# A message-passing layer on one core: 200 binned groups with folded units, one load a unit, and fewer passes on ScalarE

## The chip, the core and the metric
One core of a Trainium2 chip runs the whole kernel in one launch. The metric is the device time of the execution in microseconds; the median of three runs of the kernel before is 1935.99 us.

## The reference
A graph with N = 6250 nodes of 64 features and E = 206250 edges, sorted by their target `dst`; `src` is in no order. Each edge takes the node features of its `dst` and its own 64 features through two layers of 128, and the result is summed over the edges of each `src`:

```python
h = concatenate([hx[dst], edge_attr], axis=1)        # hx = relu(layernorm(x))
h = relu(h @ W1.T + b1)
h = relu(h @ W2.T + b2)
agg = segment_sum(h, src, n) / maximum(segment_sum(1, src, n), 1)[:, None]
z = relu(concatenate([hx, agg, u], axis=1) @ Wa.T + ba)
return x + z @ Wb.T + bb
```

## The kernel before, in words
**Before the loop** the nodes' part of the first layer is computed for all nodes and stored in DRAM as `p_table`; edge indices are brought into the forms that the loop reads.

**The loop** goes over 403 groups of 512 edges (four tiles of 128), one a step. For group s, `R[:, s % 8, :]` has the edges' features in its upper 64 partitions and, in the lower 64, a one-hot of the target among 64 neighbouring rows; `L[:, s % 8, :]` holds the weights and these 64 rows of `p_table`. The first layer is one fp32 matmul of 512 columns (two records in the trace, L1373) into `psL1`. ScalarE applies the ReLU (L923). In step s + 1 come four matmuls of the second layer (L1399) onto a bias seeded by ScalarE (L912), and its ReLU (L943).

What follows depends on the kind of group. There are 211 **plain** groups. VectorE builds a mask of equal sources (L1182, from rows of sources that SP loads, `src<-rows_src`), TensorE multiplies it in step s + 2 (L1389), so that each edge holds the sum over its tile's edges of the same source; ScalarE evacuates into one of four buffers `scat` (L931), once the scatters of the plain group four back have landed; VectorE sets the indices (L1187, L1190), and GpSimd issues four indirect DMAs that add rows into one of four sets `sums` in DRAM (L821). Each waits for the previous one into its set.

The 192 **binned** groups are the odd ones from 3 to 385. A source belongs to one of 49 bins (its remainder by 49); a tile has four places for each bin and 60 places for what overflows. The placement comes from a one-hot of bins (L1175), a rank matmul (L1417, `psRank`), VectorE's L1154, L1156, L1160, L1163, two small matmuls (L1432, L1434, `psOver`) and L1140 into `perm`. In step s + 2 TensorE places each tile's edges with two matmuls (`bin_tile`, L1350), tiles 0 and 1 before the second layer of the next group and tiles 2 and 3 behind it; ScalarE evacuates each tile by itself (`evac_slots`, L906) into `slot_sb`. SP stores it (L606, L607) into `slots[n, place, :]`. The overflow rows of two binned groups are added up (L1204, L1205, `V`, L1410, L1170, L1423, L965) and go out in one indirect DMA (L809), 96 in all.

**Units.** The binned groups form blocks of 32 (six blocks). A unit is two bins of one block, 25 units a block. SP loads it (L629), one DMA a bin: 128 partitions (32 groups x 4 places) of four tiles x 130 values. VectorE makes a one-hot of each row's source, one operation a bin and tile (L1215, `oh2`), TensorE multiplies (`add_up`, L1361, eight matmuls, 16 records) and VectorE adds the result into `acc` (`add_unit`, L1131 for the first block, L1134 for the others). `unit_steps` gives the steps: for blocks 0 to 4 one unit at an even step, 25 spread over the steps to the next block's first unit (64 steps, for the last of them 60); the first is nine steps behind the last group of its block (step 74 for block 0). Block 5 runs from step 390, three units one a step and then two a step to 403. A unit of step s is loaded in SP's step s (one later in the last block), its one-hots are made in VectorE's step s - 1, and it is added in VectorE's step s + 1. Loads go into three buffers, six in the last block (`BX`, in space that is free by then).

**The destination one-hot** is made on VectorE for plain groups (L1147, one operation, step s - 1). For binned groups ScalarE makes it in two passes (L954, the absolute value of the difference, and L959, ReLU of one minus it, step s - 2).

**The order** on every engine is the program's order, written by hand as one function `step(s)` for each, and engines wait for one another by semaphores. On TensorE a step is: first layer of s, sum or tiles 0 and 1 of s - 2, second layer of s - 1, tiles 2 and 3, the matmuls for the overflow rows and ranks, the unit, the two small matmuls for the overflow places. On VectorE: L1140, L1147, ranks and places, L1170, L1175, L1182, indices, L1204 and L1205, the add of the unit before, the one-hots of the next.

**The finish.** When all scatters have landed SP and ScalarE load the four sets in pieces (`regA<-sums`), VectorE adds them and `acc` (L1231, L1233, L1234), and the update layers and the store follow. TensorE first waits for all units' adds and then issues the node features' part of the update layer (L1452).

The branch `general == 1` is for inputs that break the assumptions on windows and places; with these inputs it is not taken.

Of the kernel before, what the change touches and what calls it, by code (L numbers as in the profile page):

```python
# [5 lines left out]
P = 128  # L6
TILE = 128
TPG = 4
# [39 lines left out]
LAST_SORTED = 386  # L48
# [9 lines left out]
BLOCK = 32  # L58
QLAG, VPRE, VREAD, VBC, VMASK, VSUM, VLAG = 6, 3, 7, 6, 7, 8, 5
ODD = 196  # L60
NS = ODD * TPG
# [3 lines left out]
ROUNDS = [[(0, 4), (4, 5)]] + [[(a, a + 4), (a + 4, a + 8)] for a in range(5, 45, 8)] + [[(45, 49)]]  # L65
# [8 lines left out]
UNIT_RING, SPARE = 3, 3  # L74
TAIL_LAG, TAIL_LEAD = 5, 1


def is_sorted(g):
    return 2 < g < LAST_SORTED and g % 2 == 1

# [11 lines left out]
BLOCKS = [BINNED[k:k + BLOCK] for k in range(0, NH, BLOCK)]  # L92
# [42 lines left out]
def unit_steps():  # L135
    at = {}
    firsts = [block[-1] + VREAD + 2 for block in BLOCKS[:-1]] + [BLOCKS[-1][-1] + TAIL_LAG]
    for k in range(len(BLOCKS) - 1):
        for q in range(UNITS):
            span = firsts[k + 1] - firsts[k]  # L140
            s = firsts[k] + 2 * (span * q // (2 * UNITS))
            at.setdefault(s, []).append((k, q))
    alone = VSUM - TAIL_LAG
    for q in range(UNITS):
        s = firsts[-1] + (q if q < alone else alone + (q - alone) // 2)
        at.setdefault(s, []).append((len(BLOCKS) - 1, q))
    return at
# [3 lines left out]
STEPS = max(max(UNITS_AT) + TAIL_LEAD + 1, NG + VSUM + 1)  # L151
# [5 lines left out]
UNIT_NO = {kq: n for n, kq in enumerate(kq for s in sorted(UNITS_AT) for kq in UNITS_AT[s])}  # L157


LOADS_AT = {}  # L160
for at, units in sorted(UNITS_AT.items()):
    for k, q in units:
        LOADS_AT.setdefault(at + (TAIL_LEAD if k == len(BLOCKS) - 1 else 0), []).append((k, q))
TAIL_UNIT = len(UNIT_NO) - UNITS
PAIRED = TAIL_UNIT + VSUM - TAIL_LAG


def buffer_of(m):
    return m % UNIT_RING if m < TAIL_UNIT else (m - TAIL_UNIT) % (UNIT_RING + SPARE)


def users(m):
    return [n for n in range(m + 1) if buffer_of(n) == buffer_of(m)]


def added_for(m):
    return m if m <= PAIRED else m - 1
# [6 lines left out]
def arrived(m):  # L184
    parts = {n: unit_bins(q)[1] for (_, q), n in UNIT_NO.items()}
    return sum(parts[n] for n in users(m))


# [8 lines left out]
def build(nc, x, src_cols, dst_cols, src_rows, dst_rows, ea, u, w1t, b1, w2t, b2, wat, ba, wbt, bb, out):  # L197
# [13 lines left out]
    with ctx:  # L211
# [67 lines left out]
        def loaded(m):  # L279

            n = buffer_of(m)
            return BR[:, n, :, :, :] if n < UNIT_RING else BX[:, n - UNIT_RING, :, :, :]
# [1244 lines left out]
```

## Time and profile before
| what | us |
|---|---|
| median of three runs | 1935.99 |
| lowest, highest | 1925.9, 1936.51 |
| span of the profiled execution | 1917.2 |
| busy in it: TensorE | 1737.8 |
| ScalarE | 1433.6 |
| VectorE | 1289.0 |
| GpSimd | 1528.8 |

The profile is of one execution; the page gives its span from the first to the last instruction, and no time of its own beside it. The median of the runs is 18.8 us above the span. PE is TensorE's matmul, PEld its weight load, DVE VectorE, ACT ScalarE, POOL GpSimd, SP the engine that issues most DMAs. In rows, `<-` leads from what is written to what is read, and behind a time of idleness to what ended it. An fp32 matmul shows as two records, and a few records can be missing.

### The profile page before, as it was taken

How to read it: one execution, taken by the hardware profiler on the slowest of the kernel's cores; microseconds unless marked ns; L12 is line 12 of the kernel's file. 1: busy time of each engine (PE TensorE's matmuls, PEld its weight loads, DVE VectorE, ACT ScalarE, POOL GpSimd, SP SyncE). 2: the span in 40 equal slices, each digit the busy share in tenths (PEclk: the TensorE clock that was granted, in tenths of full speed). 3: DMA queues.
4: the chain of work that ended last, by engine and by line, in shares of the span. 5: the costliest groups of instructions: out<-in, count | busy, mean ns of one | idle time of the engine just before them, and what ended most of it. 6: DMA issues, size and time to landing. Idle time of an engine off the chain costs nothing.

```text
span 1917.2 us, 43265 instructions
## 1 busy us (share of the span) xinstructions
PE 1737.8 (91%) x12472; PEld 1470.5 (77%) x12472; DVE 1289.0 (67%) x4235; ACT 1433.6 (75%) x2975; POOL 1528.8 (80%) x991
## 2 busy tenths in 40 slices
PE   6898888999999999999999999999999999978837
PEld 4677666888888888888788788888888888867725
DVE  8565555667767676777776777777776676756727
ACT  4788887878888877788788787878877877862306
POOL 8488888888888888888888888888888888888850
PEclk8999999999999999999999999999999999998969
DMA  9988888999999999999999999999999999999856
GB/s 329 269 166 151 151 151 149 187 198 193 198 192 192 201 190 196 201 192 192 200 197 187 185 199 198 200 193 197 204 194 198 191 199 199 197 183 234 176 116 217
DMA packets 319400, 372.10 MB, mean 194 GB/s; under 512 B 42272, under 2 KB 203264, under 8 KB 318528
## 3 DMA queue, kind: packets, MB, share of 16 engines
q1 hardware_dynamic: 182400, 305.12, 55.6%
q0 software_dynamic: 135360, 62.15, 34.4%
q8 instruction: 110, 1.80, 0.4%
q10 hardware_dynamic: 1408, 2.03, 0.3%
q14 instruction: 122, 1.00, 0.1%
HBM read 203.87 MB, written 159.27 MB: 189 GB/s over the span
## 4 chain that ended last, share of the span: by engine, by line
POOL 44%; issue 19%; PE 17%; DMA 11%; DVE 5%; ACT 3%; SPq 1%; ACTq 0%; POOLq 0%; DVEq 0%
POOL sums L821 39%; DMA sums<-regA,idx 7%; POOL sums L809 5%; PE bank L1361 4%; PE bank L1350 4%; PE bank L1399 3%; PE bank L1373 3%; DVE regC L1215 2%; PE bank L1389 1%; DMA regC<-slots 1%; DMA regA<-sums 1%; DMA sums<-vscat,vidx 1%; ACT regA L931 1%; DVE regC L1182 1%; PE bank L1275 1%
## 5 line engine op out<-in xcount | busy, mean ns | idle before, releaser
L821 POOL DMA_INDIRECT sums<-regA,idx x844 | 1333.9, 1580 | 291.7 <-issue 244.4
L1350 PEld LDWEIGHTS bank<-h,regC 128*128 128x128 f32 x3072 | 389.0, 194 | 183.1 <-ACT h L943 134.0
L1350 PE MATMUL bank<-h,regC 128*128 128x130 f32 x3072 | 421.7, 281 | 63.0 <-ACT h L943 62.8
L1373 PE MATMUL bank<-regA,L 128*128 128x512 f32 x806 | 435.8, 623 | 4.6 <-DVE regA L1147 3.0
L1399 PE MATMUL bank<-w,h 128*128 128x128 f32 x3224 | 431.3, 277 | 0.0
L923 ACT ACTIVATE h<-bank,b1c 128x512 f32<-128x512 f32 x403 | 275.7, 684 | 198.0 <-PE bank L1373 193.1
L1399 PEld LDWEIGHTS bank<-w,h 128*128 128x128 f32 x3224 | 398.0, 194 | 1.1 <-ACT h L923 0.6
L1215 DVE TENSOR_SCALAR regC<-lows,regC 128x128 f32<-128x128 f32 x1176 | 257.7, 315 | 147.6 <-DMA regC<-slots 124.0
L1361 PE MATMUL bank<-regC 128*128 128x129 f32 x2352 | 298.3, 281 | 34.4 <-issue 19.0
L943 ACT ACTIVATE h<-bank 128x512 f32<-128x512 f32 x403 | 240.9, 598 | 111.1 <-PE bank L1399 107.2
L1361 PEld LDWEIGHTS bank<-regC 128*128 128x128 f32 x2352 | 277.2, 193 | 41.8 <-issue 38.1
L1389 PEld LDWEIGHTS bank<-h,regC 128*128 128x128 f32 x1688 | 223.1, 192 | 102.2 <-issue 98.7
L906 ACT ACTIVATE regC<-bank 128x260 f32<-128x260 f32 x768 | 270.4, 385 | 4.5 <-PE bank L1350 3.9
L912 ACT ACTIVATE bank<-b2b 128x512 f32<-128x512 f32 x403 | 242.4, 602 | 11.2
L1389 PE MATMUL bank<-h,regC 128*128 128x130 f32 x1688 | 224.7, 276 | 0.5 <-ACT h L943 0.5
L1182 DVE TENSOR_TENSOR regC<-src,srcF 128x512 f32<-128x512 uint16 x211 | 146.4, 694 | 99.7 <-DMA src<-rows_src 95.1
L1156 DVE TENSOR_TENSOR regC<-bank,ranks 128x784 f32<-128x784 f32 x192 | 184.5, 961 | 0.0
L931 ACT ACTIVATE regA<-bank 128x520 f32<-128x520 f32 x211 | 126.4, 599 | 71.7 <-DMA sums<-regA,idx 54.6
L809 POOL DMA_INDIRECT sums<-vscat,vidx x96 | 153.0, 1594 | 31.2 <-issue 26.8
L1154 DVE TENSOR_REDUCE rank<-bank 128x4 f32<-128x196 f32 x192 | 68.3, 356 | 140.0 <-PE bank L1417 137.6
L1140 DVE TENSOR_TENSOR regC<-bank,overs 128x240 f32<-128x240 f32 x192 | 77.0, 401 | 115.8 <-PE bank L1434 114.9
L954 ACT ACTIVATE regA<-dstR,oh_bias 64x512 f32<-64x512 uint8 x192 | 137.6, 717 | 4.9
(142 smaller groups left out, 1540.3 us busy)
## 6 DMA issues: line engine op xcount, KB each, us to landing
regC<-slots SPq DMA_DIRECT2D x294, 260.0 KB, 5.6
regA<-in_ea SPq DMA_DIRECT2D x202, 256.0 KB
slots<-regC SPq DMA_DIRECT2D x192, 260.0 KB
src<-rows_src SPq DMA_DIRECT2D x107, 256.0 KB
slots<-regC SPq DMA_DIRECT2D x192, 138.1 KB
sums<-regA,idx POOLq DMA_INDIRECT x844
dstR<-rows_dst SPq DMA_DIRECT2D x101, 128.0 KB
sums<-zeros SPq DMA_DIRECT2D x20, 645.0 KB, 7.0
```

The lines of the kernel that those rows point to most:

```text
L809: nc.gpsimd.indirect_dma_start(out=sums[k], out_offset=bass.IndirectOffsetOnAxis(ap=vidx[:, j % 6:j % 6 + 1], axis=0), in_=vscat[:, j % 4, ...
L821: nc.gpsimd.indirect_dma_start(out=sums[k], out_offset=bass.IndirectOffsetOnAxis(ap=idx[:, n % RING, t:t + 1], axis=0), in_=scat[:, n % 4, ...
L906: nc.scalar.activation(slot_sb[:, n % 2, :, t, :], psSlot(t), ACT.Copy).then_inc(slot_ready, 1)
L912: nc.scalar.activation(psL2(g % 2).rearrange("p (t f) -> p t f", t=TPG), b2b[:, :].unsqueeze(1).broadcast_to([P, TPG, H]), ACT.Copy).then_ ...
L923: nc.scalar.activation(h1[:, s % 2, :], psL1(s % 2), ACT.Relu, bias=b1c[:, :]).then_inc(h1_ready, 1)
L943: nc.scalar.activation(h2[:, g % 2, :, 0:H], psL2(g % 2).rearrange("p (t f) -> p t f", t=TPG), ACT.Relu).then_inc(h2_ready, 1)
L1215: made = VE.tensor_scalar(oh2[0:rows, m % 2, i, t, :], lows[0:rows, i, :], loaded(m)[0:rows, i, t, C:W], -float(b), ALU.subtract, ALU.is_e ...
L1350: last = T.matmul(psSlot(t)[:, k, :], place, h2[:, g % 2, t, :], start=True, stop=True)
L1361: last = T.matmul(psUnit(m)[:, i * C:(i + 1) * C], oh2[0:rows, m % 2, i, t, :] if not general else zeros[0:rows, 0:LO], loaded(m)[0:rows, ...
L1373: T.matmul(psL1(s % 2), L[:, s % RING, :], R[:, s % RING, :], start=True, stop=True).then_inc(l1_done, 1)
L1389: last = T.matmul(bank[:, 6 + t // 2, (t % 2) * W:(t % 2 + 1) * W], S[:, n % 4, t, :], h2[:, g % 2, t, :], start=True, stop=True)
L1399: last = T.matmul(psL2(g % 2)[:, t * H:(t + 1) * H], h1[:, g % 2, t * TILE:(t + 1) * TILE], w2[:, :], start=False, stop=True, skip_group_c ...
```

## The change
- Binned are now the 200 odd groups from 3 to 401; 203 groups stay plain.
- Blocks are of 32 groups (four), 16 (four) and 8 (one). `FOLD` is 1, 2 and 4: the tiles of a row are folded onto partitions, so a unit of a smaller block again has 128 partitions, with two tiles or one behind each, and takes half or a quarter of the matmuls. There are 225 units.
- `unit_steps`: blocks 0 to 2 as before. From block 3 on units follow one another: a whole unit takes two steps, a half one a step, a quarter half a step, and none starts ahead of its block. So block 3 has steps 266 to 315, the four half blocks 316 to 415, the last block 416 to 428. The last two blocks are loaded a step later than the others.
- `slots` is laid out by bin, then by group and place, so that a unit's rows are contiguous, and one DMA loads both bins. The three buffers are a ring of 12 quarters; `BX` is gone.
- The unit's one-hot is one operation with two tensor operands for all tiles of a bin, two a unit.
- ScalarE evacuates two tiles of a binned group in one pass over two banks, and TensorE's third tile waits for the first pass.
- The destination one-hot is VectorE's for all groups; ScalarE's two passes go.
- Units' sums lie in one bank until step 404 and then in four in turn.

```diff
-LAST_SORTED = 386
+FIRST_SORTED, LAST_SORTED = 3, 402
...
-BLOCK = 32
+SIZES = [32] * 4 + [16] * 4 + [8]
...
-UNIT_RING, SPARE = 3, 3
-TAIL_LAG, TAIL_LEAD = 5, 1
+UNIT_RING = 3
+LATE, LATE_LAG, STEADY = 2, 5, 3
...
+BLOCKS = [BINNED[sum(SIZES[:k]):sum(SIZES[:k + 1])] for k in range(len(SIZES))]
+FOLD = [max(SIZES) // len(block) for block in BLOCKS]
...
+    late = len(BLOCKS) - LATE
+    firsts = [block[-1] + (VREAD + 2 if k < late else LATE_LAG) for k, block in enumerate(BLOCKS)]
+    for k in range(STEADY):
         for q in range(UNITS):
             span = firsts[k + 1] - firsts[k]
...
+            at.setdefault(firsts[k] + 2 * (span * q // (2 * UNITS)), []).append((k, q))
+    due = 4 * firsts[STEADY]
+    for k in range(STEADY, len(BLOCKS)):
+        due = max(due, 4 * firsts[k])
+        for q in range(UNITS):
+            at.setdefault(due // 4, []).append((k, q))
+            due += 8 // FOLD[k]
...
+APART = NG + 2
+ALONE = sum(len(units) for s, units in UNITS_AT.items() if s < APART)
...
+            at.setdefault(s + (1 if k >= len(BLOCKS) - LATE else 0), []).append((k, q))
...
-    slots = nc.dram_tensor("slots", (NH, PLACES, TPG * W), f32, kind="Internal").ap()
+    slots = nc.dram_tensor("slots", (NBIN, NH * CAP, TPG * W), f32, kind="Internal").ap()
...
-            return bank[:, 0 if m >= PAIRED and m % 2 else 1, 0:PAIR * C]
+            return bank[:, 1 if m < ALONE else 2 + (m - ALONE) % 4, 0:PAIR * C]
...
-                    sp.dma_start(slots[n, 0:HEAD, :], slot_sb[OVER:P, n % 2, 0, :, :].rearrange("p t c -> p (t c)")).then_inc(slot_out[n % 2], 16)
+                    sp.dma_start(slots[0:HEAD // CAP, CAP * n:CAP * (n + 1), :], slot_sb[OVER:P, n % 2, 0, :, :].rearrange("p t c -> p (t c)")).then_inc(slot_out[n % 2], 16)
...
-                    for i in range(nb):
-                        sp.dma_start(loaded(m)[0:CAP * len(block), i, :, :].rearrange("p t c -> p (t c)"),
-                                     slots[h0:h0 + len(block), CAP * (b + i):CAP * (b + i + 1), :]).then_inc(unit_in[buffer_of(m)], 16)
+                    wait(sp, unit_done, UNIT_FREED[m])
+                    r0, r1 = (CAP * FOLD[k] * h for h in (BINNED_NO[block[0]], BINNED_NO[block[-1]] + 1))
+                    folded = slots[b:b + nb, :, :].rearrange("b r (f x) -> (r f) b x", f=FOLD[k])
+                    sp.dma_start(loaded(m)[0:r1 - r0, 0:nb, :, :].rearrange("p b t c -> p b (t c)"), folded[r0:r1, :, :]).then_inc(unit_in[UNIT_AT[m]], 16)
...
+            def evac_slots(g, pair):
+
+                n, t = BINNED_NO[g], 2 * pair
+                act.wait_ge(slot_done, TPG * n + t + 2)
...
-                nc.scalar.activation(slot_sb[:, n % 2, :, t, :], psSlot(t), ACT.Copy).then_inc(slot_ready, 1)
+                nc.scalar.activation(slot_sb[:, n % 2, :, t:t + 2, :].rearrange("p h t c -> p t h c"), psSlots, ACT.Copy).then_inc(slot_ready, 1)
...
-                    nc.scalar.activation(R[D:P, g % RING, :], dB[D:P, i % 2, g % GPP, :], ACT.Abs, bias=oh_bias[D:P, :]).then_inc(oh_far, 1)
...
-                    nc.scalar.activation(R[D:P, g % RING, :], R[D:P, g % RING, :], ACT.Relu, bias=1.0, scale=-1.0).then_inc(oh_act_ready, 1)
...
-                if 0 <= g < NG and not is_sorted(g):
+                if 0 <= g < NG:
...
-                        for t in range(TPG):
-                            made = VE.tensor_scalar(oh2[0:rows, m % 2, i, t, :], lows[0:rows, i, :], loaded(m)[0:rows, i, t, C:W], -float(b), ALU.subtract, ALU.is_equal)
+                        made = VE.scalar_tensor_tensor(out=oh2[0:rows, m % 2, i, 0:size, :], in0=loaded(m)[0:rows, i, :, C:W].broadcast_to([rows, size, LO]), scalar=float(b),
+                                                       in1=lows[0:rows, i, :].unsqueeze(1).broadcast_to([rows, size, LO]), op0=ALU.subtract, op1=ALU.is_equal)
...
-                if t >= 2:
-                    pe.wait_ge(slot_ready, TPG * n + t - 1)
+                if t == 2:
+                    pe.wait_ge(slot_ready, 2 * n + 1)
...
-                wait(pe, acc_ready, added_for(m))
+                wait(pe, acc_ready, m if m < ALONE else m - 3)
```

## Rows read from the trace of the kernel before

**Rows 1.** The head of the page.
```profile
span 1917.2 us, 43265 instructions
```

**Rows 2.** The chain of waits, 1000 to 1060 us: start us, us, what.
```profile
1013.75 1.54 POOL sums L821
...
1015.60 1.55 POOL sums L821
```

**Rows 3.** Groups by line, whole span: count, busy us, mean ns, idle before.
```profile
L821 POOL DMA_INDIRECT sums<-regA,idx x844 | 1333.9, 1580 | 291.7 <-issue 244.4 <-DVE idx L1190 25.5 <-DMA sums<-regA,idx 12.8
...
L906 ACT ACTIVATE regC<-bank 128x260 f32<-128x260 f32 x768 | 270.4, 385 | 4.5 <-PE bank L1350 3.9
L1215 DVE TENSOR_SCALAR regC<-lows,regC 128x128 f32<-128x128 f32 x1176 | 257.7, 315 | 147.6 <-DMA regC<-slots 124.0 <-PE bank L1361 22.9
...
L1182 DVE TENSOR_TENSOR regC<-src,srcF 128x512 f32<-128x512 uint16 x211 | 146.4, 694 | 99.7 <-DMA src<-rows_src 95.1
L954 ACT ACTIVATE regA<-dstR,oh_bias 64x512 f32<-64x512 uint8 x192 | 137.6, 717 | 4.9
L931 ACT ACTIVATE regA<-bank 128x520 f32<-128x520 f32 x211 | 126.4, 599 | 71.7 <-DMA sums<-regA,idx 54.6 <-PE bank L1389 12.7 <-DMA sums<-vscat,vidx 3.3
...
L959 ACT ACTIVATE regA<-regA 64x512 f32<-64x512 f32 x192 | 120.3, 627 | 4.6
L1147 DVE TENSOR_SCALAR regA<-dstR,oh_row 64x512 f32<-64x512 uint8 x211 | 109.7, 520 | 31.1 <-DMA dstR<-rows_dst 24.4
...
L1205 DVE TENSOR_TENSOR vpre<-vhalf 60x130 f32<-60x130 f32 x192 | 55.3, 288 | 6.6
L1134 DVE TENSOR_TENSOR regB<-regB,bank 128x258 f32<-128x258 f32 (+1 forms) x125 | 51.3, 417 | 2.0 <-PE bank L1361 2.0
```

**Rows 4.** Windows: PE, PEld, DVE, ACT, POOL busy us (count), PEclk, DMA share, GB/s.
```profile
100.00:350.00 250.00, 214.91 (x1459) 175.73 (x1460) 135.76 (x413) 205.46 (x433) 209.47 (x134) 0.96 0.84 154
350.00:1700.00 1350.00, 1300.03 (x9619) 1117.67 (x9618) 959.63 (x3293) 1088.57 (x2270) 1124.05 (x712) 0.99 0.94 196
```

**Rows 5.** Waits of the vector engine, 350 to 1700 us: us in total, times, longest.
```profile
DVE regC L1215 <- DMA regC<-slots: 108.6, 88, 3.2
DVE regC L1140 <- PE bank L1434: 106.2, 84, 2.4
DVE regC L1182 <- DMA src<-rows_src: 89.1, 61, 3.1
DVE rank L1154 <- PE bank L1417: 35.6, 35, 2.8
```

**Rows 6.** Timeline of PE over one pair of steps: start us, us, what.
```profile
999.99 1.05 PE L1373 MATMUL bank<-regA,L 128*128 128x512 f32 x2
...
1002.66 1.95 PE L1361 MATMUL bank<-regC 128*128 128x129 f32 x16
1004.45 0.17 PE L1432 MATMUL bank<-over,prefix 128*128 128x4 bf16 x1
...
1008.46 1.02 PE L1373 MATMUL bank<-regA,L 128*128 128x512 f32 x2
```

**Rows 7.** Timeline of the end of the scatters and the start of the finish.
```profile
1830.08 0.60 ACT L931 ACTIVATE regA<-bank 128x520 f32<-128x520 f32 x1 [3.27 <-PE bank L1389]
...
1832.14 5.33 PE L1452 MATMUL bank<-hT,wax 128*128 128x256 f32 x16 [2.11 <-issue]
...
1853.86 1.54 POOL L821 DMA_INDIRECT sums<-regA,idx  x1 [0.30 <-issue]
...
1862.34 1.23 DVE L1231 TENSOR_TENSOR regC<-regA 128x1032 f32<-128x1032 f32 x1 [31.21 <-DMA regA<-sums]
```

**Rows 8.** DMA queue q1, 1100 to 1600 us: packets, MB, share of 16 engines.
```profile
q1 hardware_dynamic: 50591, 80.43, 57.0%
```

**Rows 9.** The same queue, 1864 to 1870 us, sums loaded alone.
```profile
q1 hardware_dynamic: 596, 2.16, 95.1%
```

**Rows 10.** The same queue, 1905 to 1917 us, output stored alone.
```profile
q1 hardware_dynamic: 720, 0.56, 14.2%
```

More of the change, by code:

```diff
@@ L176, in added_for, with load_steps, ring_table @@
-def added_for(m):
-    return m if m <= PAIRED else m - 1
+UNIT_OF = {n: kq for kq, n in UNIT_NO.items()}
+APART = NG + 2
+ALONE = sum(len(units) for s, units in UNITS_AT.items() if s < APART)
+def load_steps():
+    at = {}
+    for s, units in sorted(UNITS_AT.items()):
+        for k, q in units:
+            at.setdefault(s + (1 if k >= len(BLOCKS) - LATE else 0), []).append((k, q))
+    return at
+LOADS_AT = load_steps()
+QUARTERS = UNIT_RING * TPG
+def ring_table():
+    place, freed, arrived, at = {}, {}, {}, 0
+    last, begun = {}, [0] * QUARTERS
+    for m in range(len(UNIT_OF)):
+        k, q = UNIT_OF[m]
+        size = TPG // FOLD[k]
+        mine = range(at, at + size)
+        place[m] = at
+        freed[m] = max((last[c] + 1 for c in mine if c in last), default=0)
+        for c in mine:
+            last[c] = m
+        begun[at] += 1
+        arrived[m] = begun[at]
+        at = (at + size) % QUARTERS
+    return place, freed, arrived
@@ L197, in build @@
+assert HEAD % CAP == 0 and LO * NBIN == NKEPT >= N and OVER + PLACES == PW and 2 * OVER <= P and NH == 2 * NV and NG + max(VSUM, VLAG) < STEPS and NH == sum(SIZES)
+assert NBIN == BA * BA and PACK * BA <= P and NS == NPACK * PACK and PARTS[-1][1] == NPACK and (FIRST_SORTED - 1) * TPG + 2 * NS <= NT and all(len(units) == 1 for s, units in UNITS_AT.items() if s < APART)
 def build(nc, x, src_cols, dst_cols, src_rows, dst_rows, ea, u, w1t, b1, w2t, b2, wat, ba, wbt, bb, out):
@@ L584, in _ @@
                         i = s // GPP
-                        wait(sp, oh_ready, sum(1 for g in range(GPP * (i - 1)) if not is_sorted(g)))
-                        wait(sp, oh_act_ready, sum(1 for g in range(GPP * (i - 1)) if is_sorted(g)))
+                        wait(sp, oh_ready, GPP * (i - 1))
                         sp.dma_start(dB[D:P, i % 2, :, :].rearrange("p b e -> p (b e)"), rows_dst[i].partition_broadcast(P - D)).then_inc(dB_in[i % 2], 16)
@@ L1366, in step @@
                 if s < NG:
-                    pe.wait_ge(oh_ready, sum(1 for g in range(s + 1) if not is_sorted(g)))
-                    wait(pe, oh_act_ready, sum(1 for g in range(s + 1) if is_sorted(g)))
+                    pe.wait_ge(oh_ready, s + 1)
                     pe.wait_ge(ea_in[(s // 2) % 4], 16 * (s // RING + 1))
```

102 lines of the change are left out of this document (27 added, 75 removed).

## The prediction

> **What bounds the kernel now.** I read the head of the page first [rows 1]: one profiled execution with a span of 1917.2 us. The page gives no time of that execution beside the span, so I take the 18.8 us between it and the median of the three runs shown (1935.99) as what lies around it; the runs spread over 10.6 us. Then the chain of waits. It shows GpSimd's indirect accumulating DMAs one behind the other: one starts at 1013.75 and the next at 1015.60, so a scatter costs 1.85 us of GpSimd (1.54 busy and 0.30 that the profile calls issue) [rows 2]. The groups by line count 844 of them at L821 [rows 3]; with the 96 of L809 there are 940, and 940 x 1.85 = 1739 us of the 1917. A pair of steps (one plain group, one binned) has 4 + 1/2 scatters, so GpSimd alone asks 4.5 x 1.85 = 8.33 us for it. The windows show whether the loop runs at that [rows 4]: before any unit is added, 134 scatters in 250 us are 29.8 pairs of 8.40 us; with units 712 in 1350 us are 158.2 pairs of 8.53 us. There TensorE is busy 1300 of 1350 us, VectorE 960 and ScalarE 1089. So GpSimd sets the pace, 0.2 us a pair is lost to others, and TensorE is nearly as full, which matters as soon as the change gives it more.
>
> The waits of the vector engine say how it stands in the same stretch [rows 5]: 108.6 us for units' loads and 89.1 for source rows, that is 197.7 / 158.2 = 1.25 us a pair for DMAs, and 106.2 + 35.6 for TensorE, 0.90 a pair. Its own work is 959.6 / 158.2 = 6.07.
>
> TensorE's timeline over one pair [rows 6] goes from one L1373 at 999.99 to the second next at 1008.46: 8.47 us without a visible hole, with one unit in it (1002.66 to 1004.45, 1.79 us). A block of 32 spreads 25 units over 32 pairs, 0.78 a pair, so the average content is 8.47 - 0.22 x 1.79 = 8.08.
>
> **The change, part by part.**
> Eight plain groups become binned: 8 x 4 scatters go and 4 per-pair scatters come, 28 fewer, 28 x 1.85 = 51.8 us off GpSimd [rows 2]. This is the gain. The last plain sum is evacuated at 1830.08 and the last scatter ends at 1853.86 + 1.54 = 1855.4, 25.3 us later [rows 7]; after the change these stand at 1803.6 and 1778.3 if nothing else becomes late. The finish begins on VectorE at 1862.34, 6.9 us behind the last scatter, and lasts 54.8 us; that part is not changed.
>
> The tail of units. By the step table the 25 units of the first block of 16s run from step 316, one a step, and so on; those of the fourth run from 391 to 415, those of the block of 8 two a step from 416 to 428, while the edges end at 402. Behind the evacuation of the last plain sum (step 404) some 12 half units and 25 quarter units remain. I price a unit on VectorE: two one-hot operations and one add of 0.417 (L1134) [rows 3]. The new one-hot has two tensor operands; the nearest row for 512 elements is L1182 with 694 ns, for 256 L1134 with 417, for 128 L1205 with 288. A whole unit is then 2 x 0.694 + 0.417 = 1.81, a half one 1.25, a quarter one 0.99. TensorE needs 0.9 and 0.45 for the last two, so VectorE paces the tail: 12 x 1.25 + 25 x 0.99 = 40 us, with 3 for the first and last links. It ends at 1778.3 + 43 = 1821.5, where the scatters would have let the finish begin at 1803.6 + 6.9 = 1810.5: 11 us given back. The bounds are 0 (the units keep up with the 25 us of scatters) and 30 (each unit also waits for its load). The first matmuls of the finish on the node features, 5.33 us at 1832.14 [rows 7], lay under the scatters and now follow the last unit: I add 1.
>
> The dense stretch. The whole units of block 4 run one a pair from step 266 to 316 and the half units two a pair to 402, 25 + 43.5 = 68.5 pairs with one unit's worth of matmuls each instead of 0.78. TensorE's content rises from 8.08 to 8.47 [rows 6], now above GpSimd's 8.33. From below, a pair costs 8.47, less than today's 8.53; from above, today's whole distance of pace and content (0.45) stays and it costs 8.92. I take 8.8, nearer the upper end, because two engines with the same load don't hide each other's jitter: (8.8 - 8.53) x 68.5 = 18.5 us, between -4 and +27. The eight more binned groups are within these pairs.
>
> ScalarE loses both passes of the destination one-hots (717 + 627 ns, 192 times, 258 us) and evacuates slots in 400 passes of about 0.6 (L931 is the same shape of read) for 768 that were busy 270 [rows 3]: 30 us less. It was not what bound, so most of that is worth nothing. What it may give is part of the 0.2 us a pair lost between steps 74 and 266 (96 pairs): between 0 and 19 us, I take 6. The new evacuation waits for two tiles instead of one; behind it in ScalarE's queue stand h2's evacuation and then the second pair, and TensorE's third tile waits for the first pair. The second layer's matmuls between tiles two and three (as many as half a unit's, 0.9 us) cover its 0.6, with little to spare; if not, the loss is up to 0.1 us a pair, and it lies in the upper bound above.
>
> VectorE takes the destination one-hots of the binned groups: 200 x 0.520 (L1147) = 104 us. A whole unit's one-hots go from 8 x 0.219 = 1.75 (257.7 / 1176) to 1.39. Over all: one-hots 196 x 0.694 + 196 x 0.417 + 49 x 0.288 = 232 us instead of 257.7, and 75 more adds of 0.417, 31 us. VectorE ends near 1400 us busy, hidden beside GpSimd and TensorE as long as a pair leaves it room. In the half-unit stretch its work is 6.07 - 0.78 x 2.17 + 0.52 + 2 x 1.25 = 7.40 us of 8.8.
>
> The Trainium skill speaks against the one-hot edit (VectorE: DVE Perf Modes, section The perf-mode tier table): an fp32 operation with a scalar on SBUF runs at two elements a cycle and one with two tensors at one, so folding four of the first into one of the second throws the faster mode away. By the cost table of that page (section The TRN2 errata) I estimate (58 + 64) / 0.96 = 127 ns for the old operation, 1.0 us for eight, and a whole unit would cost VectorE 0.37 us more than before instead of 0.36 less. The trace has the old operation at 219 ns, so the row decides, and at neither price does VectorE pass TensorE.
>
> The loads. One DMA of two bins replaces two; SP issues 225 instead of 294, and none of its waits is new, apart from the late blocks, whose first load stands one step behind the last slot store. A folded load moves half (or a quarter) of the bytes in packets of 1040 (or 520) bytes instead of 2080. Does a packet cost by its bytes? Queue q1 took 57.0% x 500 x 16 / 50591 = 90 ns for 1590 bytes in the loop [rows 8], 95.1% x 6 x 16 / 596 = 153 ns for 3.6 KB alone [rows 9] and 14.2% x 12 x 16 / 720 = 38 ns for 0.78 KB alone [rows 10]: by its bytes, nearly. So the fold costs nothing, and 0.22 more units a pair add (0.94 - 0.84) / 0.78 x 0.22 = 0.03 to a DMA share of 0.94 [rows 4]. The other bound is a rival below. The new layout of the slots keeps each row of 2080 bytes whole; I take nothing. The eight more prologue tiles cost below 1 us.
>
> **The sum.** 1917.2 - 51.8 + 11 + 1 + 18.5 - 6 = 1889.9 of span, and 18.8 around it: 1909 us.
>
> **The rivals.**
> A: GpSimd still paces the whole loop and TensorE's extra hides, because its holes are taken from waits for the scatters (evacuations wait for landings at L931). Then only the tail counts: 1917.2 - 51.8 + 12 = 1877, time 1896, and with all of ScalarE's relief (19) 1877. For it speaks that the loop without units runs at 8.40, against it that TensorE has 50 us of holes in 1350.
> B, slower: VectorE becomes the bound in the half-unit stretch. TensorE's unit of a step waits for the add of the unit before, which stands last but one in VectorE's step, behind the destination one-hot it has been given. If its waits are latencies of loads and of rank matmuls that stay as they are, a pair costs 7.40 + 1.25 + 0.90 = 9.55: 43.5 x 1.02 = 44 us, with 7 for the 25 pairs before them. 1917.2 - 51.8 + 12 + 51 = 1928, time 1947. It passes today's time when a half-unit pair costs over 9.28. Against it: such waits shrink when VectorE comes later.
> C, slower: a packet under load costs 90 ns whatever its size. 2 x 256 packets a pair for 0.78 x 256 are 312 more, 312 x 0.09 / 16 = 1.8 us onto a DMA load of 0.94 x 8.53 = 8.0: 9.8 a pair, 43.5 x 1.27 + 7 = 62, time about 1958. Rows 9 and 10 speak against it.
>
> **How the numbers follow.** My sum 0.45, A 0.26, B 0.20, C 0.09. A change of about 1% (19 us) is what a measurement of this kernel can tell from none. My sum has +/-15 of its own around 1909, so two thirds of it is faster by over 1% (0.30); with A that is 0.56. The other third, half of B and a third of C are within 1%: 0.26. The rest, 0.18, is slower. The range takes in most of A and the foot of B and C: 1880 to 1952.
>
> **What would show it.** Right: 912 scatters 1.85 apart, L954, L959 gone, L1147 with 403 instructions of 0.52; the last scatter near 1804 to 1822; behind it a stretch with VectorE near full and units only; L1215 at 694, about 420 and 290 ns; pairs of 8.4 to 8.5 us before step 266 and of 8.7 to 8.9 behind it. Wrong: pairs over 9.2 with long waits of L1215 for slots (B, C; C with q1 over 70 ns for its smaller packets), or a pace that never leaves 8.5 (A), or a tail beyond 60 us between the last edge step and the finish.

## The result: 403 us slower, through one line of the layout

The changed kernel takes 2334.4 us (median of four runs, 2333.1 to 2335.3) beside 1931.2 (1925.9 to 1936.5) for the kernel before: a ratio of 1.2105, 95% interval 1.207 to 1.214. I had forecast 1909. The profiled execution took 2334.44 us for a span of 2332.4, so 2 us lie around the span.

The page of the changed kernel: head and busy times, two rows of the DMA part, the chain that ended last, and groups.

```profile
span 2332.4 us, 42606 instructions
...
PE 1913.0 (82%) x12676; PEld 1572.2 (67%) x12676; DVE 1404.9 (60%) x3823; ACT 1171.6 (50%) x2226; POOL 1486.0 (64%) x963
...
q1 hardware_dynamic: 201120, 310.57, 44.6%
...
SPq 53%; DMA 22%; PE 10%; issue 7%; DVE 7%; ACT 1%; DVEq 0%; ACTq 0%
...
L824 POOL DMA_INDIRECT sums<-regA,idx x812 | 1280.3, 1577 | 307.9 <-issue 276.1
...
L909 ACT ACTIVATE regC<-bank 128x520 f32<-128x520 f32 x400 | 241.6, 604 | 428.1 <-DMA slots<-regC 237.5
L812 POOL DMA_INDIRECT sums<-vscat,vidx x100 | 164.8, 1648 | 451.7 <-ACT vscat L955 417.2
L1203 DVE SCALAR_TENSOR_TENSOR regC<-regC,lows 128x512 f32<-128x512 f32 (+2 forms) x441 | 212.3, 524 | 393.7 <-DMA regC<-slots 393.3
...
L1136 DVE TENSOR_SCALAR regA<-dstR,oh_row 64x512 f32<-64x512 uint8 x403 | 208.7, 518 | 287.2 <-DMA dstR<-rows_dst 276.8
```

The edits did what they say: 912 scatters, no ScalarE passes for one-hots, 403 one-hots on VectorE at 0.52 us, as in [rows 3]. No engine is full. Every engine waits for DMAs: VectorE 393 us for units' loads and 277 for targets, ScalarE 238 for the slot stores. The chain, which before ran through GpSimd's scatters [rows 2], is now more than half "SPq": SyncE's issuing. Yet the DMA engines look idler than before. The window over the loop, changed kernel:

```profile
core 0: us, PE busy (x) PEld busy (x) DVE busy (x) ACT busy (x) POOL busy (x), PEclk, DMA share, GB/s
350.00:1780.00 1430.00, 1192.28 (x8099) 987.61 (x8098) 844.51 (x2295) 727.96 (x1384) 940.33 (x594) 0.96 0.74 156
```

594 scatters at 4.5 a pair are 132 pairs of 10.83 us, at a mean DMA share of 0.74. The kernel before had 8.53 us at 0.94 [rows 4]. A queue that holds up its issuer while the mean engine is a quarter idle suggests that the work is uneven. The view of one tile, `slots`, shows where. Changed kernel (ns min/median/max of an issue):

```profile
L613 SPq DMA_DIRECT2D slots<-regC x200: 629/729/779, 77.2 to 2227.0; - x100
L614 SPq DMA_DIRECT2D slots<-regC x200: 553/3209/5394, 78.0 to 2227.7; - x100
...
DMA to landing us min/median/max: 2.0/9.5/13.5
```

and the kernel before:

```profile
L606 SPq DMA_DIRECT2D slots<-regC x192: 298/508/1296, 76.9 to 1715.4; - x192
L607 SPq DMA_DIRECT2D slots<-regC x192: 338/349/1084, 77.4 to 1716.0; - x192
...
DMA to landing us min/median/max: 4.0/5.6/7.1
```

L613 is the first store, rows OVER to P, 68 of them, and L614 the second, of 128 rows. SyncE stays 3.2 us (median) in the issue of L614, once a pair, where the kernel before took 0.35 (L607). The timeline of SyncE in the changed kernel shows what stands behind:

```profile
1505.08 0.73 SPq L613 DMA_DIRECT2D slots<-regC  x1
1505.86 4.63 SPq L614 DMA_DIRECT2D slots<-regC  x1
1510.54 0.60 SPq L587 DMA_DIRECT2D regA<-in_ea  x1
```

The loads of edge features, targets and units all queue behind it.

**The theory** that the experiments test: the source of this store is 68 partitions, and its destination was 68 rows (`slots[n, 0:68, :]`) and is now 17 bins of 4 (`slots[0:17, 4n:4n+4, :]`). 17 and 68 have no common divisor up to 16 other than 1, so all 68 rows of 2080 bytes go through one of the 16 DMA engines. Before, 68 and 68 share 4. Bytes and rows of the store are the same. The Trainium skill states the rule (DMA: Bandwidth & Descriptors, section Why a DMA increments its semaphore by 16 and not by 1): the number of engines is the largest k up to 16 that divides the slowest dimension other than 1 of both sides. No view of the profile tells the 16 engines apart. The rivals: the new layout spreads the writes badly in DRAM whatever the number of engines; or the folded loads cost it (rival C of the prediction); or the loop has too many DMAs.

### The profile page after: what moved, and what is told of

Its sections match the earlier page's. It is cut to its first block, busy times and chain, and to the rows that moved or that the text cites. A ratio compares the mean times of both kernels' runs of the same rounds, so it can differ in the third digit from the quotient of the medians.

```text
span 2332.4 us, 42606 instructions
## 1 busy us (share of the span) xinstructions
PE 1913.0 (82%) x12676; PEld 1572.2 (67%) x12676; DVE 1404.9 (60%) x3823; ACT 1171.6 (50%) x2226; POOL 1486.0 (64%) x963
## 3 DMA queue, kind: packets, MB, share of 16 engines
q8 instruction: 113, 1.85, 0.3%
## 4 chain that ended last, share of the span: by engine, by line
SPq 53%; DMA 22%; PE 10%; issue 7%; DVE 7%; ACT 1%; DVEq 0%; ACTq 0%
SPq L614 17%; DMA regC<-slots 11%; SPq L599 9%; SPq L600 7%; DMA slots<-regC 7%; SPq L622 5%; SPq L587 4%; SPq L613 4%; DMA src<-rows_src 3%; SPq L633 3%; PE bank L1361 2%; PE bank L1350 2%; SPq L594 2%; SPq L606 2%; PE bank L1339 1%
## 5 line engine op out<-in xcount | busy, mean ns | idle before, releaser
L824 POOL DMA_INDIRECT sums<-regA,idx x812 | 1280.3, 1577 | 307.9 <-issue 276.1
L1339 PEld LDWEIGHTS bank<-h,regC 128*128 128x128 f32 x3200 | 410.5, 193 | 347.2 <-ACT regC L909 247.2
L1339 PE MATMUL bank<-h,regC 128*128 128x130 f32 x3200 | 451.9, 285 | 218.2 <-ACT regC L909 215.7
L1361 PE MATMUL bank<-regA,L 128*128 128x512 f32 x806 | 478.3, 678 | 7.6 <-DVE regA L1136 2.4
L909 ACT ACTIVATE regC<-bank 128x520 f32<-128x520 f32 x400 | 241.6, 604 | 428.1 <-DMA slots<-regC 237.5
L1203 DVE SCALAR_TENSOR_TENSOR regC<-regC,lows 128x512 f32<-128x512 f32 (+2 forms) x441 | 212.3, 524 | 393.7 <-DMA regC<-slots 393.3
L1136 DVE TENSOR_SCALAR regA<-dstR,oh_row 64x512 f32<-64x512 uint8 x403 | 208.7, 518 | 287.2 <-DMA dstR<-rows_dst 276.8
L1350 PE MATMUL bank<-regC 128*128 128x129 f32 x2450 | 327.7, 284 | 51.6 <-DVE regB L1123 32.4
L1350 PEld LDWEIGHTS bank<-regC 128*128 128x128 f32 x2450 | 301.7, 198 | 65.3 <-issue 48.5
L1377 PEld LDWEIGHTS bank<-h,regC 128*128 128x128 f32 x1624 | 245.3, 215 | 124.0 <-issue 117.1
L1377 PE MATMUL bank<-h,regC 128*128 128x130 f32 x1624 | 242.1, 297 | 0.0
L1361 PEld LDWEIGHTS bank<-regA,L 128*128 128x128 f32 x806 | 131.6, 205 | 23.8 <-issue 6.1
```

What stands on the lines that cost most here:

```text
L824: nc.gpsimd.indirect_dma_start(out=sums[k], out_offset=bass.IndirectOffsetOnAxis(ap=idx[:, n % RING, t:t + 1], axis=0), in_=scat[:, n % 4, ...
L909: nc.scalar.activation(slot_sb[:, n % 2, :, t:t + 2, :].rearrange("p h t c -> p t h c"), psSlots, ACT.Copy).then_inc(slot_ready, 1)
L1203: made = VE.scalar_tensor_tensor(out=oh2[0:rows, m % 2, i, 0:size, :], in0=loaded(m)[0:rows, i, :, C:W].broadcast_to([rows, size, LO]), sc ...
L1339: last = T.matmul(psSlot(t)[:, k, :], place, h2[:, g % 2, t, :], start=True, stop=True)
L1350: last = T.matmul(psUnit(m)[:, i * C:(i + 1) * C], oh2[0:rows, m % 2, i, t, :] if not general else zeros[0:rows, 0:LO], loaded(m)[0:rows, ...
L1361: T.matmul(psL1(s % 2), L[:, s % RING, :], R[:, s % RING, :], start=True, stop=True).then_inc(l1_done, 1)
```

## The experiments

Each time is a median beside the runs of the kernel before on the same chip (medians 1927 to 1931). I call the first one the repaired kernel; most others start from it. The cuts show the lines of the edit alone; where a third store is added, the waits for the stores' semaphore count 48 a pair in place of 32. Four to ten runs stand behind each median, and the runs of one kernel spread over 3 to 12 us (those of the kernel before over some 20). The repaired kernel and experiments 7, 9 and 13 ran on different chips, and the kernel before differs by up to 3 us between these chips. So a step of 11 us between two of them is more than either's spread, but the intervals of their ratios overlap.

**1. The changed kernel, first store in 16 bins and 1 bin.**
```diff
-sp.dma_start(slots[0:17, CAP * n:CAP * (n + 1), :], slot_sb[OVER:P, ...])
+sp.dma_start(slots[0:16, CAP * n:CAP * (n + 1), :], slot_sb[OVER:OVER + 64, ...])
+sp.dma_start(slots[16:17, CAP * n:CAP * (n + 1), :], slot_sb[OVER + 64:OVER + 68, ...])
```


> The changed kernel with its first slot store of 17 bins x 4 places cut into 16 bins and 1 bin, layout and everything else as changed. Theory 'one DMA engine' (17 bins against 68 partitions leave no common divisor of 16 or less, so the store's 68 rows all go through one of 16 DMA engines, which becomes the bound): the second store's 3.2 us on SP falls below 0.8, pairs of steps go from 11.2 us to 8.4 to 9.0, time 1890 to 1970. Rival 'layout' (four-row pieces 1.66 MB apart are slow to write or to issue in themselves): nothing moves, 2280 to 2350. Rival 'the other edits' (merged evacuation, VectorE's new work): also 2280 to 2350.

Measured: 1906.9 us, ratio 0.987 (0.983 to 0.992). 427.5 us go with one DMA more a pair. The tile `slots` of this kernel:

```profile
L614 SPq DMA_DIRECT2D slots<-regC x200: 490/520/581, 78.4 to 1809.5; - x100
L615 SPq DMA_DIRECT2D slots<-regC x200: 557/583/907, 79.0 to 1810.1; - x100
...
  DVE regC L1204: 4.1, 5
...
DMA to landing us min/median/max: 3.4/4.8/7.5
```

The issue behind the 16 bins takes 0.52 us, and VectorE's wait for units' loads is 4.1 us in all (before 124.0). So neither the layout in DRAM nor the folded loads nor the number of DMAs was the cause: both are in here, with one DMA more a pair.

**2. The changed kernel with the old layout of the slots** and two folded loads a unit:
```diff
-slots = nc.dram_tensor("slots", (NBIN, NH * CAP, TPG * W), ...)
+slots = nc.dram_tensor("slots", (NH, PLACES, TPG * W), ...)
...
-sp.dma_start(loaded(m)[0:r1 - r0, 0:nb, :, :]..., folded[r0:r1, :, :])
+for i in range(nb):
+    sp.dma_start(loaded(m)[0:rows, i, :, :]..., slots[h0:h0 + len(block), ...].rearrange("h r (f x) -> h (r f) x", f=FOLD[k]))
```


> The changed kernel with the slots laid out by group as before, stores as before, and so two loads a unit, folded from the old layout; all other edits kept. 'One DMA engine': the 68-row store is on 4 engines again, 1890 to 1970. 'Layout': the same, 1890 to 1970. 'The other edits': stays at 2280 to 2350.

Measured: 1975.8 us, 1.024 (1.020 to 1.029). The collapse is gone here too, but this is 69 us above the repaired kernel and 6 above the range on record; VectorE waits 152.5 us for units. Experiment 6 splits the 69.

**3. The kernel before, first store in 67 rows and 1.** Nothing else of the change is in it.
```diff
-sp.dma_start(slots[n, 0:HEAD, :], slot_sb[OVER:P, ...])
+sp.dma_start(slots[n, 0:67, :], slot_sb[OVER:OVER + 67, ...])
+sp.dma_start(slots[n, 67:68, :], slot_sb[OVER + 67:OVER + 68, ...])
```


> The kernel before with its first slot store of 68 rows cut into 67 rows and 1 row, old layout. 'One DMA engine': 67 has no divisor of 16 or less but 1, so 67 rows of 2080 bytes go through one engine, and the kernel before is slowed to 2200 to 2350, with the second store long on SP. 'Layout' and 'the other edits': one more small DMA a pair, 1930 to 1945.

Measured: 2324.6 us, 1.204 (1.199 to 1.209): 396 us, nearly the whole loss, made in the old layout by a number of rows that has no divisor up to 16 but 1. Its chain, the tile `slots` and the window over the loop repeat the picture:

```profile
SPq 72%; issue 9%; DMA 8%; PE 6%; POOL 3%; DVE 1%; ACT 1%; ACTq 0%; POOLq 0%; DVEq 0%
```
```profile
L606 SPq DMA_DIRECT2D slots<-regC x192: 272/470/514, 77.1 to 2112.3; - x192
L607 SPq DMA_DIRECT2D slots<-regC x192: 364/2904/4358, 77.6 to 2112.8; - x192
```
```profile
350.00:1780.00 1430.00, 1197.61 (x8069) 989.94 (x8068) 798.95 (x2734) 948.43 (x1923) 941.70 (x597) 0.96 0.73 155
```

**4. The kernel before, 64 rows and 4**, the same edit with other numbers, for the price of the extra DMA and of more even engines.

> The kernel before with its first slot store cut into 64 rows and 4 rows. 'One DMA engine', in its general form: 68 rows went through 4 engines, 17 rows each; now 4 each plus 1 on four of them, so the DMA waits of VectorE fall and the time is between 1 per cent faster and the same, 1912 to 1932. 'Layout' and 'the other edits': one more issue, 1930 to 1945.

Measured: 1921.0 us, 0.996 (0.993 to 0.998). A third store costs nothing; 64 rows on 16 engines for 68 on 4 give about 8 us.

**5. The kernel before, 47 rows and 21.** By the theory 47 rows go to one engine and 21 to seven, three each: 50 rows on the fullest if both DMAs begin at the same engine (and 68 in experiment 3). That they do is stated by the same section of the Trainium skill for this kind of queue; no run here shows it. The experiment tells "one engine is slow by its load" from "any such store is slow".

> The kernel before with its first slot store cut into 47 rows (one DMA engine) and 21 rows (7 engines, 3 each): the busiest engine carries 50 of these rows in place of 68. 'The engine's load is the bound': 67 rows made a pair of steps 10.6 us, of which 67 x about 0.09 are these packets, so 17 fewer take 1.5 us off, 9.1 a pair, 192 x 0.6 above the kernel before: 2020 to 2070. 'It is the mere use of one engine' (latency of the store or its issue, however many rows): 2200 to 2330.

Measured: 2042.6 us, 1.060 (1.054 to 1.066). It is the load:

```profile
L607 SPq DMA_DIRECT2D slots<-regC x192: 270/1068/2484, 78.5 to 1833.8; - x192
```

The traces count the engines more directly. Each part of a DMA that lands is recorded as an increment of its semaphore; the loop's loads of 64 and 128 rows, 16 engines by the rule, show 12.9 to 16.0 increments each, since some records are missing. All stores of a pair (that of 128 rows is always among them) show together:

| kernel | rows of the first store | increments a pair | by the rule |
|---|---|---|---|
| before | 68 to 68 | 20.7 | 4 + 1 + 16 = 21 |
| changed | 17 bins from 68 | 17.9 | 1 + 1 + 16 = 18 |
| repaired | 16 bins, 1 bin | 34.8 | 16 + 4 + 1 + 16 = 37 |
| experiment 3 | 67, 1 | 19.6 | 1 + 1 + 1 + 1 + 16 = 20 |
| experiment 4 | 64, 4 | 35.5 | 16 + 4 + 1 + 16 = 37 |
| experiment 5 | 47, 21 | 25.5 | 1 + 1 + 7 + 1 + 16 = 26 |

The last column takes one increment more for each store on fewer than 16 engines, which these counts suggest and nothing else here shows.

Over 192 pairs the excess is (2324.6 - 1928.3) / 192 = 2.06 us with 67 rows and (2042.6 - 1928.5) / 192 = 0.59 with 50. The 18 rows between 68 and 50 are 1.47 us, 82 ns a row (74 if the small part goes elsewhere and it is 67 against 47), near the 90 ns of a packet (of 1590 bytes in the mean) in the loop of before [rows 8]. Carried on as a straight line, the excess reaches zero near 43 rows; no run stands there. By this estimate the full engine spends 68 x 0.082 = 5.6 of a pair's 10.8 us on this store and has 5.2 for the rest. The rest does not fit the DMA share: 0.74 x 10.83 = 8.0 us of packets' time a pair on the mean engine is more than 5.2. So a packet's time in the profile is not simply time taken from the engine, and what the full engine spends on its other packets is not shown.

The next runs price the other parts, each undone alone in the repaired kernel (1906.9 us).

**6. One load a bin for one load a unit** (the loop over `i` of experiment 2, in the new layout).

> The run with 16 and 1 bins, with each unit loaded by one DMA a bin instead of one for both, from the same new layout. 'One load a unit is what took VectorE's wait for units away' (124 us before, 4 with it): the waits come back to over 100 us and the time goes to 1950 to 1980, like the run with the old layout. 'The contiguous layout did': waits stay below 30 us and time 1900 to 1920.

Measured: 1943.1 us, 1.008 (1.005 to 1.010): one load a unit is worth 36 us. I had it at nothing. The time lies between the ranges of the two theories, and so do VectorE's waits for units, 59.1 us (4.1 in the repaired kernel, 152.5 in experiment 2). Up to 1480 us the scatters are as many as in the repaired kernel (471 and 122 for 470 and 122 in 350 to 1250 and 1250 to 1480 us), and from 1480 to 1780 there are 141 for 150: the loss lies where the half units come. The other 33 us of experiment 2 belong to the old layout together with its first store in one piece of 68 rows; no run parts these two.

**7. One evacuation a tile for one a pair of tiles.**
```diff
-nc.scalar.activation(slot_sb[:, n % 2, :, t:t + 2, :]..., psSlots, ACT.Copy).then_inc(slot_ready, 1)
+nc.scalar.activation(slot_sb[:, n % 2, :, t, :], psSlot(t), ACT.Copy).then_inc(slot_ready, 1)
```


> The run with 16 and 1 bins, with ScalarE evacuating each tile of a binned group by itself as before (768 + 32 passes in place of 400). By my prediction this edit was worth nothing to speak of, since ScalarE doesn't bound: 1900 to 1915. Rival, the merged pass is a new wait of TensorE's third tile: 1885 to 1900. Rival, ScalarE's relief is what the gain rests on: above 1920.

Measured: 1895.8 us, 0.982 (0.976 to 0.988). The merged evacuation costs 11 us. In the whole run GpSimd waited 23.4 us for the evacuations of pair sums (`vscat`) in the repaired kernel and 5.7 here. ScalarE itself waited 86.5 us (301 times) for TensorE's tiles in front of the merged pass and 3.9 us (11 times) in front of the single ones. TensorE shows no wait of its third tile for ScalarE in either, so the time fell into the range of the rival, but the wait that the rival named is not the one that the rows show.

**8. The destination one-hots of binned groups on ScalarE again**, in two passes.

> The run with 16 and 1 bins, with the destination one-hots of binned groups on ScalarE again in two passes. Theory 'VectorE is near its bound in the half-unit stretch': taking 0.52 us a pair off it gives 5 to 25 us, 1882 to 1902. Rival 'ScalarE's latency holds the loop' (its freedom is what pays for the denser units): 1915 to 1940. By my sum (6 us): 1910 to 1918.

Measured: 1948.8 us, 1.010 (1.004 to 1.016). Taking them off ScalarE is worth 42 us, more than the range of the rival that had the direction right (1915 to 1940). The windows tell where; 1250 to 1480 and 1480 to 1780 us of the repaired kernel, then of this one:

```profile
1250.00:1480.00 230.00, 223.21 (x1684) 195.16 (x1683) 180.36 (x497) 145.27 (x274) 192.75 (x122) 1.00 0.96 205
1480.00:1780.00 300.00, 279.48 (x2074) 242.45 (x2073) 230.99 (x671) 181.61 (x337) 238.55 (x150) 1.00 0.91 192
```
```profile
1250.00:1480.00 230.00, 218.69 (x1612) 190.37 (x1612) 158.35 (x454) 175.11 (x313) 193.73 (x120) 0.99 0.94 197
1480.00:1780.00 300.00, 258.63 (x1841) 223.45 (x1839) 189.77 (x571) 202.56 (x357) 205.99 (x130) 0.96 0.82 171
```

Up to 1480 us the scatters are nearly as many (122, 120). Then, with a unit in every step, 150 become 130: a pair takes 10.4 us for 9.0. (The half units begin at 1399 us in the repaired kernel; its scatters run 33 us behind its first layer there.) The waits of this kernel between 1480 and 1780 us name it:

```profile
POOL sums L818 <- ACT vscat L972: 54.7, 13, 6.6
...
PEld bank L1368 <- ACT vscat L972: 40.2, 14, 2.9
PE bank L1368 <- ACT vscat L972: 37.5, 14, 2.7
```

The `vscat` evacuation stands last in ScalarE's step, behind both passes. GpSimd's scatter of the pair waits for it, and so does TensorE's unit. In the repaired kernel the same three waits are 19.1, 19.8 and 16.8 us. ScalarE is busy 203 us of 300: it is late and not full.

**9. The unit one-hots in one operation a tile again**, 1225 of them.
```diff
-made = VE.scalar_tensor_tensor(out=oh2[0:rows, m % 2, i, 0:size, :], ...)
+for t in range(size):
+    made = VE.tensor_scalar(oh2[0:rows, m % 2, i, t, :], lows[0:rows, i, :], loaded(m)[0:rows, i, t, C:W], ...)
```


> The first run of this study (the changed kernel with its first slot store in two, 1906.9 us) with one edit undone: the unit one-hots are again one operation per tile (0.219 us each in the kernel before) for one per bin (0.69, 0.42 and 0.29 us). By the rows 196 x 4 + 196 x 2 + 49 = 1225 of them are 268 us of VectorE for 214 us, 54 more. Theory: VectorE waits over 1 us a pair, so it has room and the pace stays: 1902 to 1918. Rival, VectorE is the bound wherever there are units, or TensorE's unit waits for the one-hots: most of the 54 us comes out, 1940 to 1960. Rival from the table of modes (an old operation 127 ns): VectorE has 156 us instead of 214, and if it bound, the time would fall to 1860 to 1890.

Measured: 1896.1 us, 0.982 (0.978 to 0.987), outside the range of every theory on record: VectorE has more to do (1477.8 us busy for 1409.3) and the kernel is 11 us faster.

**10. The kernel before with one part alone**, all destination one-hots on VectorE (and the store in 64 rows and 4).

> The kernel before with its first slot store in 64 and 4 rows (1921.0 us as an earlier run) and one part of the change alone: all destination one-hots on VectorE, both ScalarE passes gone. Theory: the relief was worth 42 us in the changed kernel only because there every step from 1450 us on has a unit, and TensorE's unit waits for ScalarE's evacuation of the pair sum behind the pass; in the kernel before both pace and count of scatters were the same with and without the passes up to 1480 us, so little comes here: 1908 to 1922. Rival, the passes delay ScalarE's evacuations everywhere, also where GpSimd waits for them: 42 us as there, 1875 to 1895.

Measured: 1923.0 us, 0.997 (0.995 to 1.000), beside 1921.0 without it. Alone the relief is worth nothing.

**11. The kernel before with the new layout, 16 bins and 1, and one load a unit.**

> The kernel before, blocks and everything else as they were, with the new layout of the slots (first store 16 bins and 1 bin) and one load for a unit's two bins: two parts of the change without the folding. Theory: VectorE's 149.5 us of waits for units' loads all but go, but these waits lie in room that it has while GpSimd and TensorE set the pace: 1908 to 1924 beside 1921.0 for the same kernel with the old layout and its store in 64 and 4 rows. The 36 us that one load was worth in the changed kernel belong to the stretch with units each step. Rival, one load is worth those 36 us in any kernel: 1880 to 1895.

Measured: 1912.6 us, 0.991 (0.989 to 0.994): 8 us less than experiment 4 (1921.0), for layout and single load together, though VectorE's waits for units fall from 149.5 to 11.7 us. Where units come in every step the single load alone is worth 36.

**12. The kernel of experiment 7 with the evacuation of the plain sum behind that of h2.**

> The fastest kernel so far (the changed one with its first store in two and one evacuation a tile, 1895.8 us) with ScalarE's evacuation of a plain sum moved behind the evacuation of h2 in its step. There it waits 161 us between 350 and 1100 us for scatters to land, and TensorE waits 109 us for the h2 evacuations queued behind it. Theory: those waits of TensorE are what a pair loses to GpSimd's 8.33 us (209 scatters in 400 us are 8.61 a pair), so half of 0.28 us over 190 pairs comes back: 1860 to 1885. Rival, GpSimd then waits for the plain sum, which comes later by h2's evacuation of 0.6 us, or TensorE waits for the sum's bank: no change or slower, 1890 to 1925.

Measured: 1896.6 us, 0.982 (0.978 to 0.987), beside 1895.8. ScalarE's wait for landing scatters stood in front of h2, and moving it changes nothing; the rival holds.

**13. Both edits of experiments 7 and 9 undone.**

> The changed kernel with its first slot store in two, one evacuation a tile (alone 1895.8 us) and one unit one-hot per tile (alone 1896.1 us, beside 1906.9 with both edits in). Theory: the two gains come from different waits, TensorE's third slot tile behind ScalarE's pair, and its unit behind VectorE's longer step of one-hots, and add: 1882 to 1889. Rival, both only remove delays from the same chain of a pair of steps, and GpSimd's 8.33 us a pair is then what is left: 1892 to 1900.

Measured: 1885.4 us (1885.0 to 1889.5), ratio 0.979 (0.973 to 0.985). The two gains, 11.1 and 10.8 us, add to 21.9, and with both edits undone 21.5 come, so nearly all of each is there without the other. This is the fastest kernel of the study. The window over the loop, of the repaired kernel and of this one:

```profile
350.00:1780.00 1430.00, 1366.62 (x10162) 1183.54 (x10163) 1085.10 (x2973) 898.73 (x1706) 1186.24 (x740) 1.00 0.93 197
```
```profile
350.00:1780.00 1430.00, 1373.63 (x10308) 1190.63 (x10309) 1168.95 (x3780) 921.98 (x2062) 1198.94 (x752) 1.00 0.95 200
```

740 scatters become 752, a pair 8.70 us becomes 8.56. The two gains lie in different stretches, as far as one execution of each can tell. Here are 350 to 1250 us of the repaired kernel and of experiment 9:

```profile
350.00:1250.00 900.00, 863.92 (x6409) 745.92 (x6410) 673.75 (x1807) 571.84 (x1095) 754.94 (x470) 0.99 0.93 196
```
```profile
350.00:1250.00 900.00, 869.86 (x6489) 754.08 (x6490) 723.33 (x2326) 582.00 (x1110) 754.11 (x476) 0.99 0.96 198
```

From 1250 to 1780 us both have 272. Experiment 7 has 472 and 277, this one 478 and 276. At some 1.9 us a scatter six of them are 11 us and five are 10.

Why experiment 9 gains is not settled. One thing to look at is how long GpSimd's scatters are busy, repaired kernel and experiment 9:

```profile
L825 POOL DMA_INDIRECT sums<-regA,idx x812 | 1297.6, 1598 | 277.1 <-issue 235.5 <-DVE idx L1180 31.2 <-ACT regA L935 6.0
L813 POOL DMA_INDIRECT sums<-vscat,vidx x100 | 159.8, 1598 | 50.2 <-issue 26.8 <-ACT vscat L956 23.4
```
```profile
L825 POOL DMA_INDIRECT sums<-regA,idx x812 | 1288.0, 1586 | 276.4 <-issue 234.3 <-DVE idx L1180 31.3 <-ACT regA L935 3.7
L813 POOL DMA_INDIRECT sums<-vscat,vidx x100 | 160.0, 1600 | 48.9 <-issue 25.9 <-ACT vscat L956 22.0 <-DVE idx L1180 0.9
```

The same 912 scatters are busy 1457.4 us with two-tensor one-hots and 1448.0 with the old ones; in experiments 7 and 13 it is 1462.5 and 1455.4. But each is one execution, and kernels that all have the two-tensor one-hots range from 1445.1 us (the changed kernel) to 1468.3 (experiment 12), so these 9.4 and 7.1 us are not a finding. The Trainium skill (SBUF — State Buffer, section Who interferes with whom) would allow such an effect: a VectorE instruction with two SBUF inputs contends with a GpSimd instruction that reads SBUF. The same section has VectorE contend with GpSimd in its two-port modes as well, which an operation like the old one can enter, so it does not decide between the two forms. No run here shows an instruction blocked in that way, and the cause stays open.

## Why the prediction was wrong

**The step that failed** is in the paragraph on the loads: "The new layout of the slots keeps each row of 2080 bytes whole; I take nothing." Bytes and rows stayed; what changed was over how many DMA engines they go. Experiments 1 and 3 give its size from both sides: 427.5 us gone when the 17 is cut into 16 and 1, and 396 us made in the old kernel by 67 rows. The range to 1952 had no room for it, and no rival had this mechanism: C charged packets to 16 equal engines. I had also read the DMA share of 0.94 [rows 4] as the measure of the DMA side. It is a mean over 16 engines, and it fell to 0.74 when one became the bound.

**The rest of the sum** can be read in the repaired kernel. Its median of 1906.9 lies 2 us from the forecast, but by luck: errors cancel. The forecast started from 1935.99, and the later runs of the kernel before have a median of 1928.3, 8 us lower; and it took off 27.3 us where 21.4 came, 6 too many.

- What lies around the span: I took 18.8 us. It is 2 us in each execution whose time and span are both known. So the profiled execution of the kernel before took about 1919 us, 9 below that median, and the profiled one of the repaired kernel took 1910.79, the slowest of its four. The forecast of the span, 1889.9, misses the 1908.9 of the latter by 19 us, but some 13 of these are the spread of executions, at the start and at the end. The bullets below compare these two executions.
- GpSimd's 28 fewer scatters, 51.8 us: the counts are right (912), and so is the distance of 1.85.
- The tail, +11: a little more. The last scatter and the start of the finish in the repaired kernel:

```profile
1827.65 1.54 POOL L813 DMA_INDIRECT sums<-vscat,vidx  x1 [0.30 <-issue]
```
```profile
1848.98 1.23 DVE L1221 TENSOR_TENSOR regC<-regA 128x1032 f32<-128x1032 f32 x1
```
  19.8 us from the scatter's end; 6.9 + 11 = 17.9 were forecast.
- The dense stretch, 8.8 us a pair: from 1250 to 1780 us there are 272 scatters, 530 x 4.5 / 272 = 8.77. The number is right and the picture is not. Counted from the start of each group's first scatter, groups 266 to 402 take 8.84 a pair, 8.55 with whole units and 9.02 with half units; the first layer's ReLU (L927) takes 8.66 and 9.39. The half-unit stretch is beyond the upper bound of 8.92, and the engines ahead of GpSimd are slower there than GpSimd, which lived on the groups that waited for it: it was 33 us behind the ReLU of group 316 and 17 behind that of group 402. And the number stands on two covers that I had priced at almost nothing, the relief of ScalarE and the single load.
- The relief, -6: as a part alone nothing (experiment 10), but 42 us in the new kernel (experiment 8), where a unit in each step waits for ScalarE's last evacuation. Without it the half-unit stretch runs at 10.4, beyond the 9.55 of rival B, and what TensorE and GpSimd wait for there is ScalarE's last evacuation and not VectorE.
- One load a unit, taken as nothing: 36 us (experiment 6), and at most about 8 us in the kernel before (experiment 11, together with the layout). "None of its waits is new" was true and missed that DMAs were the wait most often seen in VectorE's rows [rows 5].
- The merged evacuation, "worth nothing" and up to 0.1 us a pair of loss: 11 us over 200 pairs, 0.055 each. Within the bounds, and I took the wrong end. What I had waiting was TensorE's third tile; what the rows of experiment 7 show is ScalarE waiting for the second.
- The unit one-hots: VectorE's saving came out near the forecast (0.685 us for 512 elements, 0.694 taken; two of them for eight of 273.4 / 1225 = 0.223 save 0.42 us a whole unit, 0.36 forecast), but not what it does to the kernel, where the edit costs 11 us. The 127 ns for an old one, set against the trace's 219 in the prediction, come from a row of the cost table that its own section in the Trainium skill (VectorE: DVE Perf Modes, section The TRN2 errata) calls too low for a single operation.
- The loop before the dense stretch: 8.40 to 8.50 a pair was forecast and 8.62 came, 900 x 4.5 / 470 between 350 and 1250 us; the kernel before had 473 scatters there, 8.56. With both small edits undone it is 8.47 (478 scatters). The loss of 6 us and the 6 that were not gained put the last scatter later: it starts at 1827.65, outside the 1804 to 1822 that I had given as a sign of being right.
- Two slips in the working: the tail ends at 1778.3 + 43 = 1821.3 and not 1821.5, and the chances add up to 0.28 for within 1% and 0.16 for slower, not 0.26 and 0.18.

Rival A fell: its pace of 8.40 came in none of these windows. Rivals B and C were right that the half-unit stretch is fragile; what experiments 6 and 8 show there is neither VectorE's work nor the size of packets.

## What to carry to other kernels

When a DMA's shape changes, compare the slowest dimensions of source and destination before and after, not only bytes and packet sizes: where the two counts have no common divisor from 2 to 16 (17 bins and 68 rows here, or 67 and 67), the whole transfer goes to one of 16 engines. In a profile this shows as a low mean DMA share together with long issues on the queue's engine, and the long issue is that of the DMA behind the guilty one. Price covers together with what they cover: a relief that is worth nothing in the kernel before can be worth 42 us once another edit leans on it.

## What the runs showed of the hardware that I had not expected

- One DMA a pair with all its 68 rows of 2080 bytes on one engine took the kernel from 1931 to 2334 us. Between 50 and 68 rows on the fullest engine a row costs some 82 ns of a pair, an estimate from two runs.
- The issue of the next DMA on SyncE then lasts up to 5.4 us (median 3.2), where the median is 0.35 in the kernel before and 0.52 in the repaired one.
- More VectorE work (68 us busy) in smaller operations with one tensor input made the kernel faster by 11 us; why is open.
- One DMA of 128 rows and two runs each, for two DMAs of one run, was worth 36 us at the same bytes, nearly all of it where units come in every step.
